# Decoder layer on one core: scores in three one-pass products, denominators on four column tiles with reciprocals spread by DMA

## The chip, the cores and the metric

The kernel runs on one core of a Trainium2 chip. The metric is the device time of one execution in microseconds, the median of several runs. The engines named below are TensorE (PE in the profile, its weight loads PEld), VectorE (DVE), ScalarE (ACT), GpSimd (POOL) and SyncE (SP), which here only issues DMAs. PSUM has eight banks of 512 fp32 columns.

## The reference

A decoder layer in fp32 on x of shape (4, 256, 128): local attention, cross-attention to a context of 512 tokens, and a mixture of experts. The change lies in the last two.

```python
# cross-attention: 16 heads of 64, b = 4, n = 256 queries, s = 512 keys
lat = layer_norm(latents, ln_lat_g, ln_lat_b)
ctx = layer_norm(context, ln_ctx_g, ln_ctx_b)
q = (lat @ Wq).reshape(b, n, HEADS, DHEAD).transpose(0, 2, 1, 3)
k, v = jnp.split(ctx @ Wkv, 2, axis=-1)          # then by head
k = apply_rope(k, cos[None, None], sin[None, None])
attn = jnp.einsum('bhnd,bhsd->bhns', q, k) * scale
attn = jax.nn.softmax(jnp.clip(attn, -11.0, 11.0), axis=-1)
out = jnp.einsum('bhns,bhsd->bhnd', attn, v)
return out @ Wo + bo
# mixture: 12 experts, three routings of the same address
x_addr = x_flat @ P_w.T
dw1, dw2, dw3 = (_route_dense(x_addr @ U.T, 3, 1.0) for U in (U1, U2, U3))
h = jax.nn.gelu(_apply_mixture(x_flat, dw1, W1), approximate=False)
y = _apply_mixture(h, dw2, W2) + dw3 @ b2
```

## The kernel before, in words

Everything is one program with one hand-written instruction list per engine; semaphores order them, and each engine runs its list in order. After the local attention come 32 rounds of cross-attention (`for r in range(NPAIR)`), one for each pair of heads of a batch entry (8 pairs each, `PPB`), then 24 expert steps (12 of the first, 12 for the second weights), then the second mixture.

One round r, on each engine:

- TensorE: the scores of the next pair (`scores`, line 1171: for two context tiles and both heads a fp32 product on 64 rows, so two row tiles), a unit of values and later a unit of rotated keys for a coming group (`unit`, line 981, three one-pass products), every other round the queries of two pairs (`queries`, lines 1104 to 1106, three one-pass products), the value products of this pair (`weigh_values`, line 1188), the sum of the weights over the context (`sum_weights`, line 1198, a product with ones, one 64-column tile for each head, so that the sum stands on all 64 rows of its head), at times the output projection (`project`, line 1207), and the transposes of the keys of pair r + 3 (`turn_keys`, line 1090).
- ScalarE: the exponents (line 806), and the copies of keys and queries out of bank 6 (lines 785 and 798), which free that bank (`misc_read`).
- VectorE: `divide(r - 1)` (reciprocal of the sums, line 1596, then the product into o_t, line 1600), the clips of the next pair (line 1589), and the rope products of the round's key unit (lines 1471 and 1476), which free bank 5 for TensorE's next unit.
- GpSimd: the sums of the weights over context tiles (lines 541, 547) and the sum of the rope products (line 533).

fp32 operands are multiplied as two records each with its own weight load; operands of type fp32r in one. Where the kernel uses fp32r it keeps fp32 accuracy by three products of a rounded first part (hi) and the rest (lo): hi·hi, hi·lo, lo·hi.

From round 22 on the routing of the first half of the tokens is worked in between (`route_1`), at fixed rounds (`ROUTE`). The routed bias dw3 @ b2 is made in the expert steps by `bias`, in steps that the table `BIAS` names: a transpose of dw3 into bank 7, ScalarE's copy (line 918), and in a later step the product (line 1353). SP's list is in order too: after the loads of the start and pw, u and b2 it issues the expert weights (line 470) into a ring of four.

In `local_values` (line 1049) each of four column tiles gets two products in a row before the next tile's two:

```python
for i in range(WG):
    for half in range(2):
        mm = pe.matmul(psum[QT * i:QT * i + QT, o, at:at + G * DE]...,
                       prT[:, q:q + QT], vbd[:, NBP * b + n, :, half, :], ...)
```

Of the kernel before, what the change touches and what calls it, by code (L numbers as in the profile page):

```python
# [7 lines left out]
P = 128  # L8
# [15 lines left out]
def decoder_layer(nc, x, ctx_in, pos, a_wq, a_wk, a_wv, a_wpost, a_wrel, a_pds,  # L24
# [75 lines left out]
    with ExitStack() as ctx:  # L100
# [38 lines left out]
        def bank(i, parts=P):  # L139
# [76 lines left out]
        q_t = sb("q_t", [P, 2, QH // 2, S], F32, second)  # L216
        kT = sb("kT", [P, 3, SC], F32, second)
        e_sb = sb("e_sb", [P, ERING, 2, KH, S], F32, second)
        v_sb.append(sb("v_sb1", [P, KC, HG, DX], F32, second))
        e_part = sb("e_part", [P, 2, 2, 2, S], F32, second)  # L220
        rden = sb("rden", [P, 2, S], F32, second)
        o_t = sb("o_t", [P, 2, PPB, S], F32, second)
        second.close()
# [48 lines left out]
            xn1_done lat_in_done lat_ps lat_f_done lat_hi_done lat_lo_done bo_added             k_rot_done misc_ps misc_read score_ps exp_done  # L272
            clip_done part_done es_done pv_ps den_ps rden_done ox_done tail_ps x2_done ld_w0 ld_w1 ld_w2 ld_w3
            ld_pw ld_u ld_b2 wt_done wt_hi_done wt_lo_done rt_ps rt_done fn_done fT_ps fT_done addr_ps addr_done z_ps
            z_done fill_done top_done top3_done zr_done chosen_done zsh_done ez_done wsum_done nm_done ctx_nm_done
            dw_done pick_done spread_done gate_src_done gate_stored ld_gate0 ld_gate1 dw1_ps dw1_hi_done dw1_lo_done dw3_ps dw3_done spread_ps xe_done xe_pool_done
# [28 lines left out]
        LATENT_ROUNDS = {1: (0, 1, 2), 2: (6, 7, 8), 3: (14, 15, 16)}  # L305
# [19 lines left out]
        MISC_NO = {what: n for n, what in enumerate(MISC)}  # L325

# [10 lines left out]
        NORM_ROUND = (B - 1) * PPB - 2  # L337
        ROUTE = {"weights": 2 * NORM_ROUND, "tokens": 2 * NORM_ROUND + 2, "address": 2 * NORM_ROUND + 4, "scores": 2 * NORM_ROUND + 6,
# [16 lines left out]
        BIAS = {10: ("turn", 0), 11: ("product", 0), 13: ("turn", 1), 14: ("product", 1)}  # L355
# [18 lines left out]
        def _(sp):  # L374
# [103 lines left out]
        def _(pool):  # L478
# [110 lines left out]
            for r in range(NPAIR):  # L589
# [14 lines left out]
                if r == FILLED:  # L604
# [4 lines left out]
                    pool.tensor_tensor(pick[:, :], ident[0:SPLIT, 0:NE], ident[0:SPLIT, REST:SPLIT], ALU.add).then_inc(s["pick_done"], 1)  # L609
                    pool.wait_ge(s["pick_done"], 1)  # L610
# [18 lines left out]
        def _(act):  # L629
# [151 lines left out]
            def keys_turned(p):  # L781
# [3 lines left out]
                act.activation(kT[:, p % 3, :], bank(MISC_BANK), ACT.Copy).then_inc(s["misc_read"], 1)  # L785
# [8 lines left out]
            def queries_out(j):  # L794
# [3 lines left out]
                act.activation(q_t[:, j % 2, :, :], bank(MISC_BANK).rearrange("p (a t) -> p a t", t=S), ACT.Copy).then_inc(s["misc_read"], 1)  # L798
# [134 lines left out]
        def _(pe):  # L933
# [225 lines left out]
            def scores(i):  # L1159
# [32 lines left out]
            def sum_weights(p):  # L1192
# [4 lines left out]
                for a in range(2):  # L1197
                    mm = pe.matmul(psum[DX * a:DX * a + DX, pv_bank(p), S:2 * S], ones[:, :], e_part[:, p % 2, 0, a, :],  # L1198
                                   start=True, stop=True)
# [83 lines left out]
            for r in range(NPAIR):  # L1283
# [14 lines left out]
                if r % 2 == 0 and r // 2 + 1 < NQ:  # L1298
                    queries(r // 2 + 1)
                route_1(2 * r)  # L1300
                weigh_values(2 * r)
# [94 lines left out]
        def _(dve):  # L1396
# [154 lines left out]
            def output_bias(pair):  # L1551

                dve.wait_ge(s["ld_bo"], 16)
                for t in range(4 * pair, 4 * pair + 4):
                    dve.tensor_tensor(x_sb[:, t, :], x_sb[:, t, :], bo_all[:, :], ALU.add).then_inc(s["bo_added"], 1)  # L1555
# [20 lines left out]
            latents(0, 2)  # L1576
            local_residual(1)
            latents_lo(0)
            context_normalize(1)
            for b in range(2, B):  # L1580
                context_offset(b)
            local_normalize(4)
# [8 lines left out]
            def divide(p):  # L1591
                b, hp = divmod(p, PPB)
# [238 lines left out]
```

## Time and profile before

| | us |
|---|---|
| median of 3 runs (lowest, highest) | 453.61 (452.78, 457.39) |
| profiled execution, its own time | 453.26 |
| its span in the trace | 451.3 |
| TensorE busy | 422.7 (94%) |
| VectorE busy | 331.1 (73%) |
| GpSimd busy | 256.3 (57%) |
| ScalarE busy | 195.1 (43%) |
| mean granted clock of TensorE | 0.992 |

The span runs from the first to the last instruction of the trace; the execution's own time has some 2 us around it. Busy times are averages over stages with different limits, so the rows further down are read by stage and by round. A record of TensorE overlaps with its neighbours: its length is its latency, and the distance of two starts is what it costs in a row of them.

### The profile page before, as it was taken

The page shows a single profiled execution, that of the slowest core. Times are in us where ns is not written, and L with a number is a line of the kernel's source. Part 1 is how long each engine was busy: PE and PEld are TensorE (multiplying, and loading weights), DVE is VectorE, ACT ScalarE, POOL GpSimd, SP SyncE. Part 2 cuts the span into 40 slices and gives each one's busy share as a digit, 9 for nine tenths or more (in the row PEclk, how much of TensorE's full clock was granted, in tenths as well). Part 3 has the DMA queues.
Part 4 walks back from the last instruction along what each step waited for, and adds up shares of the span by engine and source line. Part 5 has one row for each costly group of instructions (what it writes and reads, how often), then busy time and mean ns, then how long its engine had stood idle before and what let it go on. Part 6 is the DMA issues. An engine that isn't in the chain of part 4 may idle for free.

```text
span 451.3 us, 8472 instructions
## 1 busy us (share of the span) xinstructions
PE 422.7 (94%) x3168; PEld 309.8 (69%) x3168; DVE 331.1 (73%) x692; ACT 195.1 (43%) x312; POOL 256.3 (57%) x225
## 2 busy tenths in 40 slices
PE   3998889999999999998998999999989899999996
PEld 2666666676766766666765666768756788888885
DVE  8798668989997667987685697797667861655554
ACT  6758364664654454554354363535436533100000
POOL 5758258987898768886875745677524571000000
PEclk9999999999999999999998999999999899999999
DMA  7676314000000000000000000536438640000000
GB/s 182 173 169 86 81 33 70 0 1 1 0 2 1 1 1 1 0 1 2 0 2 1 1 1 1 163 49 139 78 83 170 140 71 1 6 6 13 6 6 14
DMA packets 75434, 19.85 MB, mean 44 GB/s; under 512 B 66741, under 2 KB 73834, under 8 KB 75394
## 3 DMA queue, kind: packets, MB, share of 16 engines
q1 hardware_dynamic: 72628, 18.27, 19.1%
q10 hardware_dynamic: 2766, 1.04, 1.0%
q8 instruction: 26, 0.43, 0.4%
q14 instruction: 14, 0.11, 0.1%
HBM read 17.27 MB, written 2.02 MB: 43 GB/s over the span
## 4 chain that ended last, share of the span: by engine, by line
PE 72%; DVE 13%; issue 5%; ACT 4%; SPq 4%; DMA 1%; POOL 1%; DVEq 0%; ACTq 0%; POOLq 0%
PE psum L1188 12%; PE psum L1171 9%; PE psum L981 8%; PE psum L1371 5%; PE psum L1372 5%; PE psum L1370 5%; PE psum L1330 4%; PE psum L1332 4%; PE psum L1331 4%; PE psum L1207 3%; PE psum L1198 3%; SPq L388 3%; PE psum L1090 3%; DVE rden L1596 1%; DVE x_sb L1555 1%
## 5 line engine op out<-in xcount | busy, mean ns | idle before, releaser
L541 POOL TENSOR_TENSOR e_part<-e_sb 128x512 f32<-128x512 f32 x64 | 88.6, 1401 | 43.1 <-DVE e_sb L1589 31.1
L806 ACT ACTIVATE e_sb<-psum 128x1024 f32<-128x1024 f32 x64 | 62.2, 1021 | 16.7 <-PE psum L1171 16.7
L1188 PE MATMUL psum<-e_sb,v_sb 128*64 128x256 f32 x512 | 64.2, 391 | 0.8 <-ACT v_sb L713 0.8
L1171 PE MATMUL psum<-q_t,kT 64*128 64x256 f32 x512 | 64.2, 389 | 0.0
L1795 DVE SCALAR_TENSOR_TENSOR x_sb<-psum,dw,x_sb 128x128 f32<-128x128 f32 x96 | 33.7, 351 | 38.1 <-PE psum L1372 35.5
L1589 DVE TENSOR_SCALAR e_sb<-e_sb 128x1024 f32<-128x1024 f32 x64 | 54.0, 879 | 4.6 <-ACT e_sb L806 4.6
L1596 DVE RECIPROCAL rden<-psum 128x256 f32<-128x256 f32 x32 | 55.9, 1747 | 0.3 <-PE psum L1198 0.2
L785 ACT ACTIVATE kT<-psum 128x512 f32<-128x512 f32 x32 | 19.1, 597 | 83.1 <-PE psum L1090 82.8
L1171 PEld LDWEIGHTS psum<-q_t,kT 64*128 64x128 f32 x512 | 46.7, 186 | 9.6 <-issue 5.0
L533 POOL TENSOR_TENSOR k_rot<-rope_a,rope_b 128x512 f32<-128x512 f32 x32 | 42.2, 1321 | 18.3 <-DVE rope_b L1476 18.3
L1188 PEld LDWEIGHTS psum<-e_sb,v_sb 128*64 128x64 f32 x512 | 34.7, 138 | 23.2 <-issue 6.2
L581 POOL TENSOR_TENSOR xeT_lo<-xeT,xeT_hi 128x512 fp32r<-128x512 f32 x24 | 31.4, 1309 | 33.8 <-ACT xeT_hi L820 33.6
L547 POOL TENSOR_TENSOR e_part<-e_part 128x512 f32<-128x512 f32 x32 | 41.4, 1293 | 2.5
L1471 DVE TENSOR_TENSOR rope_a<-psum,cos_sb 128x512 f32<-128x512 f32 x32 | 22.0, 687 | 26.2 <-PE psum L981 24.1
L1330 PE MATMUL psum<-xeT_hi,w1T_hi 128*128 128x512 f32 x96 | 39.5, 412 | 0.7 <-ACT h_f L926 0.3
L1332 PE MATMUL psum<-xeT_hi,w1T_lo 128*128 128x512 f32 x96 | 38.1, 397 | 0.0
L1371 PE MATMUL psum<-w2T_lo,h_hi 128*128 128x512 f32 x96 | 38.0, 396 | 0.0
L1331 PE MATMUL psum<-xeT_lo,w1T_hi 128*128 128x512 f32 x96 | 38.0, 396 | 0.0
L1372 PE MATMUL psum<-w2T_hi,h_lo 128*128 128x512 f32 x96 | 37.8, 394 | 0.0
L1370 PE MATMUL psum<-w2T_hi,h_hi 128*128 128x512 f32 x96 | 37.3, 389 | 0.0
L981 PE MATMUL psum<-wkv_hi,ctx_hi 128*128 128x512 f32 x64 | 31.6, 494 | 4.2 <-DVE rope_b L1476 4.2
L820 ACT ACTIVATE xeT_hi<-xeT 128x512 fp32r<-128x512 f32 x24 | 15.2, 632 | 36.9 <-DVE xeT L1636 22.1
(195 smaller groups left out, 774.8 us busy)
## 6 DMA issues: line engine op xcount, KB each, us to landing
w_raw<-in_L_ffn_W_dram SPq DMA_DIRECT2D x96, 64.0 KB, 2.3
gates<-gate_dram SPq DMA_DIRECT2D x6, 768.0 KB, 4.6
ctx_sb<-in_ctx_dram SPq DMA_DIRECT2D x4, 256.0 KB, 6.0
vbd<-v_dram SPq DMA_DIRECT2D x16, 52.6 KB
v_dram<-v_tok SPq DMA_DIRECT2D x4, 136.0 KB, 2.9
raw<-in_L_xattn_Wkv_dram SPq DMA_DIRECT2D x2, 256.0 KB, 4.6
k_rot<-in_L_xattn_Wkv_dram SPq DMA_DIRECT2D x2, 256.0 KB, 4.3
k_rot<-in_L_xattn_Wq_dram SPq DMA_DIRECT2D x2, 256.0 KB, 5.5
```

Of the source, the lines that this page charges most:

```text
L541: pool.tensor_tensor(e_part[:, p % 2, half, :, :], e_sb[:, i % ERING, :, 0, :], e_sb[:, i % ERING, :, 1, :], ALU.add)\
L806: act.activation(e_sb[:, i % ERING, :, :, :].rearrange("p a k t -> p (a k t)"), psum[:, a:a + 2, :].rearrange("p a b -> p (a b)"), ACT.Exp ...
L981: mm = pe.matmul(o, c, w_[:, wc:wc + GC], start=(part == 0), stop=(part == 2))
L1171: mm = pe.matmul(psum[:, 2 * (i % 2) + a, t * S:(t + 1) * S], kT[rows, p % 3, kt * P:(kt + 1) * P], q_t[rows, j % 2, p % 2, :], start=True ...
L1188: mm = pe.matmul(psum[DX * a:DX * a + DX, pv_bank(p), 0:S], v_sb[g % 2][:, kt, 2 * pp + a, :], e_sb[:, i % ERING, a, t, :], start=(kt == 0 ...
L1330: pe.matmul(bank(c), w1T_hi[:, e, c, :], hi, start=(e == 0), stop=False)
L1331: pe.matmul(bank(c), w1T_hi[:, e, c, :], lo, start=False, stop=False)
L1332: mm = pe.matmul(bank(c), w1T_lo[:, e, c, :], hi, start=False, stop=(e == NE - 1))
L1370: pe.matmul(o, hi, w_hi, start=(c == 0), stop=False)
L1371: pe.matmul(o, hi, w_lo, start=False, stop=False)
L1372: mm = pe.matmul(o, lo, w_hi, start=False, stop=(c == HC - 1))
L1596: dve.reciprocal(rden[:, p % 2, :], psum[:, pv_bank(p), S:2 * S]).then_inc(s["rden_done"], 1)
```

## The change

1. Scores: keys and queries are kept as a first part (kT_hi, q_hi, fp32r, copied by ScalarE) and the rest (kT_lo, q_lo, made by VectorE, which then frees bank 6). Each score product becomes three one-pass products.
2. Denominators, for the first 24 pairs (`QUARTERS`): the product with ones goes to four 32-column tiles, one for each head and half of the queries, 128 columns each; VectorE takes the reciprocal of 128 columns instead of 256 (`reciprocals`), SP copies each quarter to its two places by eight DMAs, and `divide`, now after the clips, waits for them.
3. The latents of batch 2 go from rounds 6 to 8 to rounds 9 to 11; the addition of bo is one instruction for four tiles, in rounds 6 and 26 instead of 5 and 18; in TensorE's round the routing products stand behind the first value products; the bias products go from steps 10, 11, 13, 14 to 13, 15, 17, 19.
4. Buffers are placed anew, and one semaphore of GpSimd goes (not shown).

```diff
-        LATENT_ROUNDS = {1: (0, 1, 2), 2: (6, 7, 8), 3: (14, 15, 16)}
+        LATENT_ROUNDS = {1: (0, 1, 2), 2: (9, 10, 11), 3: (14, 15, 16)}
+        QUARTERS = (B - 1) * PPB
-        BIAS = {10: ("turn", 0), 11: ("product", 0), 13: ("turn", 1), 14: ("product", 1)}
+        BIAS = {13: ("turn", 0), 15: ("product", 0), 17: ("turn", 1), 19: ("product", 1)}
...
+            def spread_reciprocals(p):
+
+                sp.wait_ge(s["rden_done"], p + 1)
+                if p >= 2:
+                    sp.wait_ge(s["ox_done"], p - 1)
+                for a in range(2):
+                    for h in range(2):
+                        quarter = SQ * (2 * a + h)
+                        for j in range(2):
+                            sp.dma_start(rden[DX * a + SQ * j:DX * a + SQ * (j + 1), p % 2, P * h:P * (h + 1)],
+                                         rden_q[quarter:quarter + SQ, p % 2, :]).then_inc(s["rden_spread"], 16)
+
+            for p in range(QUARTERS):
+                spread_reciprocals(p)
+
...
-                act.activation(kT[:, p % 3, :], bank(MISC_BANK), ACT.Copy).then_inc(s["misc_read"], 1)
+                act.activation(kT_hi[:, p % 3, :], bank(MISC_BANK), ACT.Copy).then_inc(s["misc_hi_done"], 1)
...
-                        mm = pe.matmul(psum[:, 2 * (i % 2) + a, t * S:(t + 1) * S], kT[rows, p % 3, kt * P:(kt + 1) * P],
-                                       q_t[rows, j % 2, p % 2, :], start=True, stop=True)
+                        o = psum[:, 2 * (i % 2) + a, t * S:(t + 1) * S]
+                        hi, lo = kT_hi[rows, p % 3, kt * P:(kt + 1) * P], kT_lo[rows, p % 2, kt * P:(kt + 1) * P]
+                        pe.matmul(o, hi, q_hi[rows, j % 2, p % 2, :], start=True, stop=False)
+                        pe.matmul(o, hi, q_lo[rows, j % 2, p % 2, :], start=False, stop=False)
+                        mm = pe.matmul(o, lo, q_hi[rows, j % 2, p % 2, :], start=False, stop=True)
...
+                    if p < QUARTERS:
+                        for h in range(2):
+                            quarter = SQ * (2 * a + h)
+                            mm = pe.matmul(psum[quarter:quarter + SQ, pv_bank(p), S:S + P], ones[:, 0:SQ],
+                                           e_part[:, p % 2, 0, a, P * h:P * (h + 1)], start=True, stop=True)
+                    else:
...
-                route_1(2 * r)
                 weigh_values(2 * r)
+                route_1(2 * r)
...
+            def keys_lo(p):
+                dve.wait_ge(s["misc_hi_done"], HI_NO["keys", p] + 1)
+                if p >= 2:
+                    dve.wait_ge(s["score_ps"], 2 * (p - 1))
+                dve.tensor_tensor(kT_lo[:, p % 2, :], bank(MISC_BANK), kT_hi[:, p % 3, :].bitcast(F32), ALU.subtract).then_inc(s["misc_read"], 1)
...
             def divide(p):
                 b, hp = divmod(p, PPB)
-                dve.reciprocal(rden[:, p % 2, :], psum[:, pv_bank(p), S:2 * S]).then_inc(s["rden_done"], 1)
-                dve.wait_ge(s["rden_done"], p + 1)
+                if p < QUARTERS:
+                    dve.wait_ge(s["rden_spread"], 16 * 8 * (p + 1))
+                else:
+                    dve.wait_ge(s["rden_done"], p + 1)
...
             for r in range(NPAIR):
                 if r:
-                    divide(r - 1)
+                    reciprocals(r - 1)
+                    if r > QUARTERS:
+                        divide(r - 1)
...
+                if r % 2 == 0 and r // 2 + 1 < NQ:
+                    queries_lo(r // 2 + 1)
...
                 route_1(2 * r)
+                if r and r <= QUARTERS:
+                    divide(r - 1)
...
                     key_unit(ROUND_KEYS[r])
+                if r + 3 < NPAIR:
+                    keys_lo(r + 3)
```

What moves on VectorE, in an even and an odd round in the middle of the 32. Before, from the key unit of one round (rope_a, rope_b are the rope products) over the division and the clips (e_sb):

```order
L1471 TENSOR_TENSOR rope_a<-psum,cos_sb 128x512
L1476 TENSOR_TENSOR rope_b<-psum,sin_sb 128x8x32 x2
L1596 RECIPROCAL rden<-psum 128x256
L1600 TENSOR_TENSOR o_t<-psum,rden 128x256
L1589 TENSOR_SCALAR e_sb<-e_sb 128x1024 x2
L1471 TENSOR_TENSOR rope_a<-psum,cos_sb 128x512
L1476 TENSOR_TENSOR rope_b<-psum,sin_sb 128x8x32 x2
```

And now, with kT_lo and q_lo the rests and rden_q the half-width reciprocals:

```order
L1501 TENSOR_TENSOR rope_a<-psum,cos_sb 128x512
L1506 TENSOR_TENSOR rope_b<-psum,sin_sb 128x8x32 x2
L1611 TENSOR_TENSOR kT_lo<-psum,kT_hi 128x512
L1641 RECIPROCAL rden_q<-psum 128x128
L1634 TENSOR_SCALAR e_sb<-e_sb 128x1024 x2
L1617 TENSOR_TENSOR q_lo<-psum,q_hi 128x512
L1653 TENSOR_TENSOR o_t<-psum,rden 128x256
L1501 TENSOR_TENSOR rope_a<-psum,cos_sb 128x512
```

The division has gone from ahead of the clips to behind them and behind the rest of the queries; the rest of the keys stands between the rope products and the reciprocal.

On SP, between the loads of round 0 and the expert weights. Before:

```order
L435 DMA u_sb<-in_L_ffn_U_dram 12x64 x3
L436 DMA b_sb<-in_L_ffn_b_dram 12x128
L470 DMA w_raw<-in_L_ffn_W_dram 32x16x32 x16
L440 DMA gate_dram<-gate_src 12x512 [waits gate_src_done]
L453 DMA gates<-gate_dram 128x1536 [waits misc_ps,pv_ps,gate_stored]
```

And now (of the 24 groups of eight the first and the last):

```order
L442 DMA u_sb<-in_L_ffn_U_dram 12x64 x3
L443 DMA b_sb<-in_L_ffn_b_dram 12x128
L453 DMA rden<-rden_q 32x128 [waits rden_done]
L453 DMA rden<-rden_q 32x128 x7
...
L453 DMA rden<-rden_q 32x128 [waits ox_done,rden_done]
L453 DMA rden<-rden_q 32x128 x7
L492 DMA w_raw<-in_L_ffn_W_dram 32x16x32 x16
L462 DMA gate_dram<-gate_src 12x512 [waits gate_src_done]
```

The first sixteen weight loads, which were issued in round 0, now stand behind the last group, in round 24.

## Rows read from the trace of the kernel before

**Rows 1.** The page's busy times.

```profile
PE 422.7 (94%) x3168; PEld 309.8 (69%) x3168; DVE 331.1 (73%) x692; ACT 195.1 (43%) x312; POOL 256.3 (57%) x225
```

**Rows 2.** By stage: start:end, length, busy PE, PEld, DVE, ACT, POOL, clock, DMA share, GB/s.

```profile
73.00:257.60 184.60, 178.20 (x1271) 123.45 (x1270) 148.31 (x229) 92.12 (x136) 144.83 (x115) 0.99 0.01 2
257.60:295.60 38.00, 36.18 (x290) 25.12 (x288) 31.83 (x72) 16.39 (x23) 22.72 (x18) 1.00 0.17 50
295.60:391.00 95.40, 91.32 (x414) 71.50 (x415) 62.24 (x144) 40.85 (x74) 44.00 (x35) 0.98 0.43 86
```

**Rows 3.** Timeline of one round: start, length, engine, line.

```profile
148.91 0.69 DVE L1471 TENSOR_TENSOR rope_a<-psum,cos_sb 128x512 f32<-128x512 f32 x1 [0.41 <-PE psum L981]
149.24 2.00 PE L1171 MATMUL psum<-q_t,kT 64*128 64x256 f32 x16
149.52 0.74 DVE L1476 TENSOR_TENSOR rope_b<-psum,sin_sb 128x256 f32<-128x256 f32 x2
150.18 1.75 DVE L1596 RECIPROCAL rden<-psum 128x256 f32<-128x256 f32 x1
151.96 0.42 DVE L1600 TENSOR_TENSOR o_t<-psum,rden 128x256 f32<-128x256 f32 x1
152.30 1.28 DVE L1589 TENSOR_SCALAR e_sb<-e_sb 128x1024 f32<-128x1024 f32 x2
...
156.07 0.69 DVE L1471 TENSOR_TENSOR rope_a<-psum,cos_sb 128x512 f32<-128x512 f32 x1 [2.48 <-PE psum L981]
```

**Rows 4.** Timeline, TensorE: query products (first, last), local value products.

```profile
151.97 0.28 PE L1104 MATMUL psum<-lat_hi,wq_hi 128*128 128x256 f32 x1
...
152.55 0.28 PE L1106 MATMUL psum<-lat_hi,wq_lo 128*128 128x256 f32 x1
...
38.73 2.20 PE L1049 MATMUL psum<-vbd,prT 96*32 96x68 f32 x128 [0.33 <-ACT prT L730]
```

**Rows 5.** Groups of instructions, VectorE: busy, mean ns of one.

```profile
L1520 DVE RECIPROCAL rq<-psum 128x32 f32<-128x32 f32 x5 | 1.7, 344 | 1.6 <-PE psum L1049 1.6
...
L1596 DVE RECIPROCAL rden<-psum 128x256 f32<-128x256 f32 x32 | 55.9, 1747 | 0.3 <-PE psum L1198 0.2
...
L1622 DVE TENSOR_TENSOR w1T_lo<-psum,w1T_hi 128x512 fp32r<-128x512 f32 x12 | 8.2, 687 | 5.2 <-ACT w1T_hi L813 5.2
```

**Rows 6.** Timeline, SP's DMA issues and the last VectorE group.

```profile
63.73 0.36 SPq L436 DMA_DIRECT2D b_sb<-in_L_ffn_b_dram  x1
64.14 0.35 SPq L470 DMA_DIRECT2D w_raw<-in_L_ffn_W_dram  x1
...
7.29 0.43 SPq L402 DMA_DIRECT2D affine<-in_L_xattn_ln_ctx_g_dram  x1
7.76 0.44 SPq L402 DMA_DIRECT2D affine<-in_L_xattn_ln_ctx_b_dram  x1
...
447.80 1.51 DVE L1795 SCALAR_TENSOR_TENSOR x_sb<-psum,dw,x_sb 128x128 f32<-128x128 f32 x4 [1.24 <-PE psum L1372]
449.40 0.33 SPq L474 DMA_DIRECT2D out_dram<-x_sb  x1
```

**Rows 7.** DMA issues: count, KB each, us from issue to landing.

```profile
out_dram<-x_sb SPq DMA_DIRECT2D x8, 64.0 KB, 1.5
...
pw_sb<-in_L_ffn_P_w_dram SPq DMA_DIRECT2D x1, 32.0 KB, 2.1
```

**Rows 8.** Waits of TensorE from 295 us on, and its clock.

```profile
PE psum L1353 <- ACT dw3T L918: 1.5, 1, 1.5
PE psum L1347 <- ACT gate_src L847: 1.4, 1, 1.4
...
349.20:352.60 3.40, 1.86 (x11) 1.45 (x11) 3.04 (x5) 2.81 (x6) 1.27 (x1) 1.00 0.63 100
352.60:356.10 3.50, 3.50 (x10) 2.73 (x9) 3.40 (x8) 0.93 (x2) 2.57 (x2) 0.51 0.45 69
```

More of the change, by code:

```diff
@@ L214, in decoder_layer @@
         lat_lo = sb("lat_lo", [P, B * S], F32R, second)
-        q_t = sb("q_t", [P, 2, QH // 2, S], F32, second)
-        kT = sb("kT", [P, 3, SC], F32, second)
+        q_hi = sb("q_hi", [P, 2, QH // 2, S], F32R, second)
+        kT_hi = sb("kT_hi", [P, 3, SC], F32R, second)
         e_sb = sb("e_sb", [P, ERING, 2, KH, S], F32, second)
         v_sb.append(sb("v_sb1", [P, KC, HG, DX], F32, second))
-        e_part = sb("e_part", [P, 2, 2, 2, S], F32, second)
+        sb("awT_rest", [P, 16], F32, second)
+        kT_lo = sb("kT_lo", [P, 2, SC], F32R, second)
+        q_lo = sb("q_lo", [P, 2, QH // 2, S], F32R, second)
         rden = sb("rden", [P, 2, S], F32, second)
         o_t = sb("o_t", [P, 2, PPB, S], F32, second)
+        sb("below", [P, 7144], F32, second)
+        e_part = sb("e_part", [P, 2, 2, 2, S], F32, second)
+        rden_q = sb("rden_q", [P, 2, P], F32, second)
         second.close()
@@ L325, in decoder_layer @@
         MISC_NO = {what: n for n, what in enumerate(MISC)}
+        HI_NO = {what: n for n, what in enumerate(w for w in MISC if w[0] in ("keys", "queries"))}
         def gate_bank(n):
@@ L1553, in output_bias @@
                 dve.wait_ge(s["ld_bo"], 16)
-                for t in range(4 * pair, 4 * pair + 4):
-                    dve.tensor_tensor(x_sb[:, t, :], x_sb[:, t, :], bo_all[:, :], ALU.add).then_inc(s["bo_added"], 1)
+                ts = slice(4 * pair, 4 * pair + 4)
+                dve.tensor_tensor(x_sb[:, ts, :], x_sb[:, ts, :], bo_all[:, None, :].to_broadcast([P, 4, D]), ALU.add)
             def latents_lo(b):
@@ L1581, in _ @@
                 context_offset(b)
+            queries_lo(0)
             local_normalize(4)
@@ L1589, in clip, with reciprocals @@
                 dve.tensor_scalar(e, e, E_LO, E_HI, ALU.max, ALU.min).then_inc(s["clip_done"], 1)
-            def divide(p):
-                b, hp = divmod(p, PPB)
+            def reciprocals(p):
                 dve.wait_ge(s["den_ps"], p + 1)
@@ L1595, in divide @@
                     dve.wait_ge(s["ox_done"], p - 1)
-                dve.reciprocal(rden[:, p % 2, :], psum[:, pv_bank(p), S:2 * S]).then_inc(s["rden_done"], 1)
-                dve.wait_ge(s["rden_done"], p + 1)
+                if p < QUARTERS:
+                    dve.reciprocal(rden_q[:, p % 2, :], psum[:, pv_bank(p), S:S + P]).then_inc(s["rden_done"], 1)
+                else:
+                    dve.reciprocal(rden[:, p % 2, :], psum[:, pv_bank(p), S:2 * S]).then_inc(s["rden_done"], 1)
+            def divide(p):
+                b, hp = divmod(p, PPB)
+                if p < QUARTERS:
+                    dve.wait_ge(s["rden_spread"], 16 * 8 * (p + 1))
+                else:
+                    dve.wait_ge(s["rden_done"], p + 1)
                 if hp == 0 and b >= 2:
@@ L1709, in _ @@
             key_unit(10)
-            beside = {5: (output_bias, 0), 18: (output_bias, 1)}
+            beside = {6: (output_bias, 0), NPAIR - 6: (output_bias, 1)}
             def route_1(i):
@@ L1766, in _ @@
                 if n == 0:
+                    reciprocals(NPAIR - 1)
                     divide(NPAIR - 1)
```

26 lines of the change are left out of this document (17 added, 9 removed).

## The prediction

> **What bounds the kernel now.** I read the page's busy times first: TensorE is busy for 422.7 of 451.3 us [rows 1]. An average says little about one stage, so I then cut the span: the 24 head pairs between the value products of round 1 and those of round 25 fill 184.6 us, of which TensorE is idle for 6.4; after them come 38.0 us of attention and 95.4 us of experts [rows 2]. A round there is 184.6 / 24 = 7.69 us. The timeline of one even round [rows 3] shows who is early: VectorE starts on the key unit as soon as TensorE has made it (148.91), ends its clips near 153.6, and then waits 2.48 us for the next key unit. From rope to rope is 7.16 us, all of it TensorE. So TensorE sets the pace, and VectorE has some 2.5 us to spare. The change spends that spare time, and the question is whether it spends more.
>
> **The products (TensorE).** Scores of a pair: 16 records go as 8 pairs on two row tiles, 2.00 us from first start to last end [rows 3]. The new form has 24 one-pass products. The query products are of that kind and width: first start 151.97, last 152.55, so 0.116 us from one to the next, and 0.28 for the last [rows 4]. In pairs on the two row tiles that is 11 x 0.116 + 0.28 + 0.1 (the longer first step) = 1.66 us: 0.34 less. The sums over the context halve their columns and use four tiles, two steps in the place of two longer ones: about 0.2 less. An even round of TensorE becomes 7.16 - 0.55 = 6.6 us, an odd one about 5.9 (no queries, 6 x 0.116 less). Alone this would be worth 24 x 0.55 = 13 us.
>
> The pairing needs a choice, since three products in a row now stand on one row tile before the other tile's three. The local value products are written so as well, two products (four records) in a row on one column tile, and still 128 records of 68 columns took 2.20 us, 17 ns each [rows 4]; four in a row one after the other would take more than twice that. So tiles run on their own, and I take the full pairing. The Trainium skill (TensorE: Matmul & The Clock Gate, Part 3, The mechanism) says otherwise: matmuls start and end strictly in program order. What a failed pairing costs is worked out as a rival below.
>
> **The chain on VectorE.** In the new order VectorE does: two rope products, the rest of the keys, the half-width reciprocal, clips and the rest of the queries, then it waits for the spread reciprocals, divides, and goes to the next rope. It is in order, so the DMA trip is inside each round's loop, and nothing behind the wait can start. The parts:
> - rope products: 148.91 to 150.18, 1.27 us [rows 3];
> - rest of the keys, PSUM less SBUF, 128x512: 0.69 [rows 5], less 0.07 since VectorE's neighbours overlap (150.26 against 150.18 in rows 3): 0.62;
> - reciprocal of 128 columns: between 0.344 for 32 and 1.747 for 256 [rows 5], in a straight line 0.344 + 96 x 0.00626 = 0.95;
> - the trip: eight DMAs issued by SP one after the other. Two issues of 12 rows stand 0.41 us apart (63.73, 64.14), two of 128 rows 0.47 (7.29, 7.76) [rows 6]. The new ones have 32 rows, nearest to 12: 7 x 0.41 = 2.87. The last one lands after 1.5 (SBUF to DRAM, 64 KB) or 2.1 us (DRAM to SBUF, 32 KB) [rows 7]. No DMA of before goes from SBUF to SBUF; I take 1.5, since the 2.1 has a read of DRAM in it. Two wake-ups, SP's 0.09 (447.80 + 1.51 to 449.40, rows 6) and VectorE's, rounded to 0.1 together: 4.47;
> - the division: 151.96 to 152.30, 0.34 [rows 3].
>
> Sum: 1.27 + 0.62 + 0.95 + 4.47 + 0.34 = **7.65 us** a round. Clips (two, 1.3 us) and the query rest (0.69) lie beside the trip and cost nothing unless it is under 2 us. TensorE's 6.6 and 5.9 are shorter, so TensorE no longer sets the pace; what it gains turns into waiting for the rope. What stood after the division stays in the loop: four residual adds (0.25 each) and three latent rests (0.4 each), 2.3 us. 24 x 7.65 + 2.3 = 185.9, against 184.6: **+1.3 us**. Each 0.1 us of the trip is worth 2.4 us.
>
> The trip's price is also given by the Trainium skill (DMA: Bandwidth & Descriptors, Anatomy of one DMA): about 2.0 us fixed for any transfer, though measured on GpSimd's path. With 2.0 in the place of 1.5 the sum would be 12 us higher, an estimate from that page of the Trainium skill.
>
> **The rest.**
> - Start: the query rest (0.69) stands ahead of the first scores and the rest of keys 2 (0.69) ahead of the residual that the next unit waits for; some of it lies in idle time. +1.0, between 0 and 2.
> - Rounds 25 to 31 divide as before. TensorE saves 6 x 0.34 = 2.0; VectorE, whose routing work stands here, gets three rests of keys and one or two of queries, 2.8 us. I take 0, between -2 and +2.
> - The full-width product with bo_all becomes one instruction and stands beside the trip: 0. The w_raw loads, now behind the 24 trips on SP, are first used in round 29, some 30 us later: 0. If the trips ran over, the experts' first transposes would be late.
> - Value products ahead of the routing products: nothing to win while VectorE's loop sets the pace: 0.
> - Bias products: TensorE waits 1.4 us for the turned gates and 1.5 us for the turned bias weights [rows 8]. One step of distance becomes two, at later experts, past the busiest ScalarE stretch, so both go. Behind the second wait the granted clock is 0.51 for 3.5 us, the level of 1.2 GHz in the place of 2.4, which costs 1.7 us of full-speed work [rows 8]; in the 3.40 us ahead TensorE had been busy for 1.86. With the wait gone, that goes too. **-4.6**, between -1.5 and -4.6.
> - Clock in the rounds: TensorE now idles 1 to 1.7 us in each. The only measure of that kind is the stretch just named, 1.86 busy of 3.40, and a fall after it. If a fall comes, its 1.7 us mostly fits into TensorE's slack. +2, between 0 and 6.
>
> Sum against the profiled execution's 453.26: 453.26 + 1.3 + 1.0 - 4.6 + 2 = 453.0. The median of the runs, 453.61, is 0.35 above that execution, which I leave in the rounding: **453 us**, no change.
>
> **Rivals.**
> - A, the trip is longer, and the wait that replaces TensorE's bound is worse (slower, 0.26). Place: VectorE's division in rounds 1 to 24. With issues 0.47 apart the trip is 0.42 longer, +10 us: 463; with 2.1 us of landing as well, 5.5 us in all, +24: 477. It decides from a trip of 4.7 us on; I put it at 466. For it: of the two prices of an issue the larger is that of a full tile's 128 rows, and a landing in SBUF is the one that took 2.1. Against: the new DMAs have few rows and read no DRAM.
> - B, the trip is shorter and TensorE's gain gets through (faster, 0.23). Issues as short as SP's 0.33 [rows 6] make 2.3 us, and landing in SBUF as far below 1.5 as the other row is above it, 0.9, make a trip of 3.3 and a loop of 6.5, under TensorE's even round. Then 13 us are won in the rounds: 438 in full, 443 for half-way prices.
> - C, the row tiles don't pair (0.05). Eight groups of three then take two steps each, 16 x 0.116 + 0.38 (as above) = 2.2 us, 0.2 more than now. Rounds 1 to 24 hide it (6.6 + 0.54 is under 7.65), six later ones don't: 456. The local value products speak against it [rows 4]. It is the rule that the Trainium skill (TensorE: Matmul & The Clock Gate, Part 3, The mechanism) states.
> - D, TensorE's waits drop its clock in most odd rounds (0.09): 12 falls of 1.7 us, of which about 0.5 stays each time: 459.
>
> **Numbers.** The forecast's own case (trip 4.2 to 4.7 us) has 0.37 and spans 447 to 458. About 1% (4.5 us) is what a measurement here can tell from no change. Faster by more: all of B and a fifth of the forecast, 0.30. Slower by more: A, half of D and a little of the forecast, 0.33. Within: 0.37. For 8 in 10 the range takes in most of A and B: 440 to 471.
>
> **What would show it.** In the profile after: in rounds 1 to 24 the division waits for the DMA into rden, 1 to 3 us each time, with SP's eight issues just before; TensorE's unit of values waits for the rope products; from rope to rope 7.6 us; 24 score records in 1.7 us; half-width reciprocals near 0.95 us; no wait of TensorE in the bias products. I am wrong if the last DMA lands much sooner or later than 4.5 us after the reciprocal's end, or if the score records of the two row tiles don't start in pairs.

## The result, and the profile after

The change makes the kernel slower: **502.47 us** median of four runs (501.83 to 503.06), beside 453.74 for the kernel before on the same chip. The ratio is 1.105, 95% interval 1.100 to 1.111. The forecast was 453 with a range of 440 to 471; the measured time lies outside it. All ratios here are of undisturbed runs; the highest times of two kernels below, 470.61 and 458.97 us, are runs in a slower state of the chip. The profiled execution took 502.00 us, its span is 500.1.

These are the busy times on the page after; they answer to [rows 1].

```profile
PE 429.7 (86%) x3520; PEld 317.1 (63%) x3520; DVE 320.9 (64%) x734; ACT 197.9 (40%) x312; POOL 257.6 (52%) x225
```

No engine has much more to do. TensorE is even 7 us busier (more records, and the mean granted clock of its rounds is 0.91), yet its share falls from 94 to 86%. So something makes all of them wait. The chain of waits on the same page (share of the span, first by engine, then the first lines by line) says what:

```profile
PE 36%; SPq 22%; DVE 22%; DMA 10%; issue 7%; ACT 2%; DVEq 0%; POOL 0%
SPq L453 19%; DMA rden<-rden_q 8%; PE psum L1401 4%; PE psum L1402 4%; PE psum L1400 4%; DVE rden_q L1641 4%; PE psum L1360 4%; PE psum L1362 3%; PE psum L1361 3%; DVE rope_b L1506 3%; DVE kT_lo L1611 3%; SPq L395 3%; DVE rope_a L1501 2%; P
```

SP's issuing of the spread reciprocals (L453) and their way to landing hold 27% of the chain. They were to be some 4.5 of 7.65 us in 24 rounds. The stages, cut at the value products of rounds 1 and 25 and at the first expert product, answer to [rows 2] (start:end, length, busy times, clock, DMA share):

```profile
73.51:306.94 233.43, 186.26 (x1547) 130.16 (x1546) 128.99 (x255) 93.52 (x135) 143.07 (x115) 0.91 0.08 16
306.94:349.39 42.45, 38.04 (x338) 27.08 (x337) 36.73 (x84) 17.97 (x26) 26.04 (x20) 0.96 0.26 63
349.39:500.10 150.71, 145.96 (x658) 115.90 (x657) 93.98 (x231) 40.83 (x74) 44.35 (x34) 1.00 0.29 58
```

With the same cuts in the trace before, the gain or loss of each stage is:

| stage | before | after | difference | forecast |
|---|---|---|---|---|
| start to value products of round 0 | 66.57 | 67.02 | +0.45 | +1.0 |
| value products of round 1 to round 25 | 184.61 | 233.43 | **+48.8** | +3.3, clock included |
| round 25 to the first expert product | 38.60 | 42.45 | **+3.85** | 0 |
| experts to the end | 155.09 | 150.68 | -4.4 | -4.6 |

The whole surprise is in the rounds, 9.73 us each in the place of 7.69. One of them in the timeline answers to [rows 3]:

```profile
150.45 0.95 DVE L1641 RECIPROCAL rden_q<-psum 128x128 f32<-128x128 f32 x1
151.19 3.24 PE L1212 MATMUL psum<-e_sb,v_sb 128*64 128x256 f32 x16
151.43 4.94 SPq L453 DMA_DIRECT2D rden<-rden_q  x8
151.94 1.26 DVE L1634 TENSOR_SCALAR e_sb<-e_sb 128x1024 f32<-128x1024 f32 x2
157.57 0.42 DVE L1653 TENSOR_TENSOR o_t<-psum,rden 128x256 f32<-128x256 f32 x1 [4.37 <-DMA rden<-rden_q]
157.91 0.68 DVE L1501 TENSOR_TENSOR rope_a<-psum,cos_sb 128x512 f32<-128x512 f32 x1
158.51 0.75 DVE L1506 TENSOR_TENSOR rope_b<-psum,sin_sb 128x256 f32<-128x256 f32 x2
159.17 0.68 DVE L1611 TENSOR_TENSOR kT_lo<-psum,kT_hi 128x512 fp32r<-128x512 f32 x1
159.31 0.50 PE L1002 MATMUL psum<-wkv_hi,ctx_hi 128*128 128x512 f32 x1 [1.57 <-DVE rope_b L1506]
159.77 0.95 DVE L1641 RECIPROCAL rden_q<-psum 128x128 f32<-128x128 f32 x1
```

Read it as a circle. The reciprocal ends at 151.40; SP's eight issues fill 151.43 to 156.37; the division starts at 157.57, after VectorE has stood still for 4.37 us; then division, rope and key rest, and the next reciprocal at 159.77, 9.32 us after the last. TensorE waits for the rope (1.57 us). The value products, 1.95 us at the full 2.4 GHz in a round of the trace before, take 3.24 here: the granted clock from 151.2 to 154.4, behind a wait of TensorE, is 0.58, so most of that stretch runs at 1.2 GHz. It lies inside TensorE's own slack, since TensorE still has to wait at the end of the round. What all instructions on the spread tile show, in this one round and in the whole run (duration ns min/median/max, first and last start), is:

```profile
L453 SPq DMA_DIRECT2D rden<-rden_q x8: 507/590/592, 151.4 to 155.8; - x8
```

```profile
L453 SPq DMA_DIRECT2D rden<-rden_q x192: 507/591/1608, 73.3 to 302.5; - x192
...
  DVE o_t L1653: 97.6, 24
...
DMA to landing us min/median/max: 1.7/1.8/3.4
```

An issue takes 0.59 us, and the next one follows 0.04 later. It was to be 0.41 from start to start. All 24 divisions wait, 97.6 us together.

The forecast named its own sign of being wrong, a last landing much later than 4.5 us after the reciprocal's end; here the division starts 6.17 us after it.

The score records stand as forecast, 24 in 1.7 us, two at a time (the first three groups and the last):

```profile
156.05 0.39 PE L1194 MATMUL psum<-q_hi,kT_hi 64*128 64x256 f32 x2
156.27 0.29 PE L1195 MATMUL psum<-q_lo,kT_hi 64*128 64x256 f32 x2
156.39 0.29 PE L1196 MATMUL psum<-q_hi,kT_lo 64*128 64x256 f32 x2
...
157.45 0.29 PE L1196 MATMUL psum<-q_hi,kT_lo 64*128 64x256 f32 x2
```

In kernel.py the three products of one row tile come before the three of the other; in the trace two records of line 1194, which can only be of the two tiles, start 0.01 us apart, ahead of the second product of either. The rule that matmuls start strictly in program order (the Trainium skill, TensorE: Matmul & The Clock Gate, Part 3, The mechanism) doesn't hold between row tiles in this trace.

### The profile page after: what moved, and what is told of

Read it like the earlier page. It is cut to its first block, busy times and chain, and to the rows that moved or that the text cites. A ratio compares the mean times of both kernels' runs of the same rounds, so it can differ in the third digit from the quotient of the medians.

```text
span 500.1 us, 9474 instructions
## 1 busy us (share of the span) xinstructions
PE 429.7 (86%) x3520; PEld 317.1 (63%) x3520; DVE 320.9 (64%) x734; ACT 197.9 (40%) x312; POOL 257.6 (52%) x225
## 3 DMA queue, kind: packets, MB, share of 16 engines
HBM read 17.27 MB, written 2.02 MB: 39 GB/s over the span
## 4 chain that ended last, share of the span: by engine, by line
PE 36%; SPq 22%; DVE 22%; DMA 10%; issue 7%; ACT 2%; DVEq 0%; POOL 0%
SPq L453 19%; DMA rden<-rden_q 8%; PE psum L1401 4%; PE psum L1402 4%; PE psum L1400 4%; DVE rden_q L1641 4%; PE psum L1360 4%; PE psum L1362 3%; PE psum L1361 3%; DVE rope_b L1506 3%; DVE kT_lo L1611 3%; SPq L395 3%; DVE rope_a L1501 2%; PE psum L1212 2%; DVE e_sb L1634 1%
## 5 line engine op out<-in xcount | busy, mean ns | idle before, releaser
L563 POOL TENSOR_TENSOR e_part<-e_sb 128x512 f32<-128x512 f32 x64 | 89.9, 1424 | 43.8 <-DVE e_sb L1634 31.3
L1653 DVE TENSOR_TENSOR o_t<-psum,rden 128x256 f32<-128x256 f32 x32 | 13.6, 425 | 97.9 <-DMA rden<-rden_q 97.6
L1212 PE MATMUL psum<-e_sb,v_sb 128*64 128x256 f32 x512 | 72.4, 425 | 0.1
L806 ACT ACTIVATE kT_hi<-psum 128x512 fp32r<-128x512 f32 x32 | 19.2, 599 | 98.9 <-PE psum L1111 98.5
L1212 PEld LDWEIGHTS psum<-e_sb,v_sb 128*64 128x64 f32 x512 | 37.3, 152 | 27.7 <-issue 14.1
L1634 DVE TENSOR_SCALAR e_sb<-e_sb 128x1024 f32<-128x1024 f32 x64 | 45.0, 740 | 1.6 <-ACT e_sb L827 1.6
L1002 PEld LDWEIGHTS psum<-wkv_hi,ctx_hi 128*128 128x128 f32 x64 | 12.3, 192 | 48.4 <-DVE rope_b L1506 38.9
L1194 PE MATMUL psum<-q_hi,kT_hi 64*128 64x256 f32 x256 | 41.9, 317 | 0.3 <-DVE q_lo L1617 0.3
L1360 PE MATMUL psum<-xeT_hi,w1T_hi 128*128 128x512 f32 x96 | 38.9, 405 | 0.8 <-ACT h_f L947 0.5
L1195 PE MATMUL psum<-q_lo,kT_hi 64*128 64x256 f32 x256 | 38.5, 290 | 0.0
L1196 PE MATMUL psum<-q_hi,kT_lo 64*128 64x256 f32 x256 | 38.5, 290 | 0.0
```

The costliest lines, as they stand in the source:

```text
L563: pool.tensor_tensor(e_part[:, p % 2, half, :, :], e_sb[:, i % ERING, :, 0, :], e_sb[:, i % ERING, :, 1, :], ALU.add)\
L1002: mm = pe.matmul(o, c, w_[:, wc:wc + GC], start=(part == 0), stop=(part == 2))
L1212: mm = pe.matmul(psum[DX * a:DX * a + DX, pv_bank(p), 0:S], v_sb[g % 2][:, kt, 2 * pp + a, :], e_sb[:, i % ERING, a, t, :], start=(kt == 0 ...
L1360: pe.matmul(bank(c), w1T_hi[:, e, c, :], hi, start=(e == 0), stop=False)
L1634: dve.tensor_scalar(e, e, E_LO, E_HI, ALU.max, ALU.min).then_inc(s["clip_done"], 1)
```

## The experiments

**The theory**: eight issues of one queue, one after the other, and a landing stand inside VectorE's in-order loop and set its length. **Rivals**: the rests of keys and queries that VectorE now makes; TensorE's clock; a long landing rather than long issues.

### No quarters at all

```diff
-        QUARTERS = (B - 1) * PPB
+        QUARTERS = 0
```

With it go the DMAs, the four column tiles and the half-width reciprocals, and the division stands ahead of the clips again.

> The changed kernel with no pair in quarters: sums on 64 columns, reciprocals of 256 columns, no DMA. Theory (eight issues of SP and a landing inside VectorE's in-order loop make the 9.7 us rounds): the rounds are TensorE's again, 7.69 - 0.34 for the scores = 7.3 us or a little less, and the bias products keep their 4.6 us, so 437 to 443 us. Rival (the rests of keys and queries that VectorE now takes are what slows it): rests 0.62 + 0.7 in a loop that had 2.5 us to spare; if they were the cause the time would stay near 500. Rival (TensorE's clock falls because of three short products in the place of two): about 470.

Measured: 449.33 us (447.27 to 452.46), ratio to before 0.991 (0.987 to 0.994). The quarters as a whole cost 53 us, so neither the rests (near 500) nor the clock (470) are the cause; which part of the quarters it is, the next runs show. But the expectation was missed by 6 us at the least: the rounds 1 to 24 took 181.9 us and not 175, and the end of attention 43.0 and not 38.6. What waits for what on TensorE, in this run from 66 to 310 us (us in total, times, longest):

```profile
PE psum L1111 <- DVE q_lo L1617: 7.3, 4, 2.4
PE psum L1111 <- DVE x_sb L1660: 2.9, 1, 2.9
PE psum L1002 <- DVE rope_b L1506: 2.2, 4, 1.1
```

The first two waits are new or longer: the turned keys need the bank that the query rest frees, and in one late round they need it from a residual add that stands behind VectorE's routing work (0.5 us before). Both are followed up below.

### Dividing later

```diff
-                if r and r <= QUARTERS:
-                    divide(r - 1)
...
                 if r + 3 < NPAIR:
                     keys_lo(r + 3)
+                if r and r <= QUARTERS:
+                    divide(r - 1)
```

> Eight DMAs as in the change, but VectorE divides after the rope and the key rest, just before the next reciprocal. Then only reciprocal 0.95 + trip 6.2 + division 0.34 = 7.5 us stand in the loop, the 1.9 us of rope and key rest lie beside the trip: 24 x 1.9 to 2.2 = 46 to 53 us less than the change, 450 to 457. If SP's issues take longer when TensorE and VectorE are less idle: 460 to 470. Rival (not the place of the wait in VectorE's order, but the clock or the rests): over 490.

Measured: 461.96 us (458.77 to 464.95), ratio 1.019 (1.012 to 1.026): 40 us of the 49 come back with the same eight DMAs, by nothing but the place of the wait. The profile has the smaller wait of the division and a new one behind it, since the division also frees the bank that the next value products write:

```profile
  DVE o_t L1653: 25.1, 17
  PE psum L1212: 13.0, 12
```

From the reciprocal's end to the division's start it is 6.80 us on average, not 6.2; 0.95 + 6.80 + 0.34 = 8.09 a round, and 24 rounds took 193.6 us. So the 450 to 457 us of the theory were missed, and the time lies in the second range, 460 to 470. That range had longer issues as its reason. Against the change, whose mean is 6.49, the issues hold only 0.05 us more and the landings 0.26; why these landed later is open.

### Half of the DMAs

Only four of a pair's eight DMAs are issued from pair 2 on, and the division waits for these alone; half of rden keeps the values of pairs 0 and 1.

```diff
-                        for j in range(2):
+                        for j in range(2 if p < 2 else 1):
...
```

> From pair 2 on only four of the eight DMAs are issued (half of rden keeps values of pairs 0 and 1, so outputs differ). Theory: an issue costs 0.63 us, four less take 2.5 us out of each round: loop 7.0 to 7.3, 22 x 2.5 = 55 us less than the change, 443 to 450 us. If an issue costs what I forecast (0.41) and the rest of the trip is a fixed landing that I underrated: 22 x 1.64 = 36 less, 466. Rival (clock, rests): over 490.

Measured: 451.94 us (447.72 to 470.61), ratio 0.995 (0.992 to 0.998). Typical trips are 3.63 us, 2.54 less than the 6.17 of the change, so **one DMA less is 0.63 us less**, and it is the issues that count, not a long landing. The rounds lost 48.5 us, 22 x 2.2 and not 22 x 2.5, so the time is 2 us above the range expected: in some of them TensorE sets the pace again.

### What an issue costs, by itself

A kernel of DMAs alone, in stages of eight issues by SP and a wait.

> A kernel of DMAs alone: SP issues eight at a time and waits, SBUF to SBUF with 32, 12, 64, 128 rows of 512 bytes and 32 rows of 64 bytes, SBUF to DRAM and DRAM to SBUF with 32 rows, and one single DMA; nothing else of the reference is computed. Theory 1 (the issue's price goes by rows and by SBUF on both sides): 32 rows SBUF to SBUF 0.59 each, 12 rows 0.41, 128 rows above 0.6, and DRAM on one side cheaper at 32 rows. Theory 2 (0.59 comes from load of other engines in the full kernel): here 0.41 to 0.47 for 32 rows. Landing of the last one 1.7 to 1.9 us after its issue inside SBUF.

Measured, each row one stage; the first four are SBUF to SBUF with 32, 12, 64 and 128 rows of 512 bytes, then 32 rows of 64 bytes, then 32 rows of 512 bytes from SBUF to DRAM and from DRAM to SBUF (duration ns min/median/max):

```profile
L32 SPq DMA_DIRECT2D s<-src x8: 507/591/592, 4.4 to 8.8; - x8
L32 SPq DMA_DIRECT2D s<-src x8: 713/714/847, 10.5 to 16.0; - x8
L32 SPq DMA_DIRECT2D s<-src x8: 544/596/597, 17.8 to 22.3; - x8
L32 SPq DMA_DIRECT2D s<-src x8: 482/602/610, 24.1 to 28.5; - x8
L32 SPq DMA_DIRECT2D n<-src x8: 573/590/592, 30.4 to 34.8; - x8
L32 SPq DMA_DIRECT2D hbm<-src x8: 352/421/422, 36.5 to 39.7; - x8
L32 SPq DMA_DIRECT2D l<-in_x_dram x8: 325/422/423, 41.2 to 44.4; - x8
```

With no other engine at work an issue inside SBUF costs the same 0.591 us as in the full kernel, so it isn't load. Rows (32, 64, 128) and bytes (an eighth) move it by 2%. **With DRAM on one side it costs 0.42, with SBUF on both 0.59** (32 rows of 512 bytes). Of theory 1 the half on SBUF is right, the half on rows is wrong, and 12 rows were dearest of all. Why SBUF on both sides costs more is not shown. From the start of a stage's last issue to the next stage's first it is 1.76 us for 32 rows inside SBUF, within the 1.7 to 1.9 expected, and 1.49 to DRAM.

### Two queues

Four of a pair's DMAs are issued by ScalarE's queue, behind its copy of the value unit (and of the queries, in even rounds).

```diff
...
-                spread_reciprocals(p)
+                spread_reciprocals(sp, p, 0)
...
+                if r and r <= QUARTERS:
+                    spread_reciprocals(act, r - 1, 1)
```

> The change whole, but of the eight DMAs of a pair four are issued by SP and four by ScalarE's queue, behind its copy of the value unit. Theory (the trip is the issues of one queue, one after the other, 0.63 us each): both halves go side by side and the trip is 3.65 us as with four DMAs, the loop 7.0 to 7.7 us; 450 to 455 us. Rival (the descriptors or the engines behind them are what takes 0.6 us, whichever queue issues): trip 6.2, 500 us. In between, if ScalarE comes to its issues late: 460 to 475.

> A kernel of DMAs inside SBUF alone, nothing else of the reference is computed: eight of 32 rows to the same partitions, to the next 32, eight of 128 rows, of 12 rows, of 16 rows; then four on SP's queue and four on ScalarE's at the same time; then eight on ScalarE's alone. If each queue has its own price: 0.59 us on either, alone or side by side, and the four and four take 2.5 us together. If the queues share what takes the time: 5 us for the four and four. Same partitions or shifted ones: no difference.

Measured: 459.0 us (456.17 to 460.15), ratio 1.010 (1.007 to 1.013). Half of the trips are 3.93 to 3.97 us, so the halves do go side by side; the mean is 4.69 and the longest 7.32, where ScalarE came to its issues late. So the time lies between the two ranges expected, 450 to 455 and 460 to 475. In the kernel of DMAs alone four and four took 2.7 us together (first and second rows; the third is SP's eight to the same partitions, and eight to the next 32 partitions took the same 0.590 each):

```profile
34.95 2.41 SPq L27 DMA_DIRECT2D both<-src  x4
34.96 2.70 ACTq L27 DMA_DIRECT2D both<-src  x4
```

```profile
L27 SPq DMA_DIRECT2D same<-src x8: 586/590/592, 2.6 to 7.0; - x8
```

Spreading DMAs over engines brings no bandwidth, it only saves issue time: so says the Trainium skill (DMA: Bandwidth & Descriptors, Rules for kernel authors). Issue time was what was short here, and the trips of 3.96 us in the place of 6.17 agree.

### The scores back in fp32

The quarters and all moved products stay; the copies of keys and queries are whole fp32, and VectorE makes no rests of them.

```diff
-                        pe.matmul(o, hi, q_hi[rows, j % 2, p % 2, :], start=True, stop=False)
-                        pe.matmul(o, hi, q_lo[rows, j % 2, p % 2, :], start=False, stop=False)
-                        mm = pe.matmul(o, lo, q_hi[rows, j % 2, p % 2, :], start=False, stop=True)
+                        mm = pe.matmul(o, kT_hi[rows, p % 3, kt * P:(kt + 1) * P], q_hi[rows, j % 2, p % 2, :], start=True, stop=True)
...
```

> The change with its scores in fp32 as before (no rests of keys and queries on VectorE); quarters, DMAs and moved products stay. Theory: in the loop of reciprocal, trip, division, rope and key rest only the key rest goes, 0.62 us: 24 x 0.62 = 15 us, and the 3.9 us that the end of attention lost: 502.5 - 15 - 4 = 483 us, still 30 us slower than before. Rival (the rests and the DMAs get in each other's way): under 470. Rival (the rests cost nothing): 502.

Measured: 487.31 us (485.69 to 488.7), ratio 1.073 (1.070 to 1.077). The rounds lose 12.1 us of 233.4, the stretch after them 2.7: the rests are the smaller part. From the division to the next reciprocal's end it is 0.60 us less each time, near the 0.62 of the forecast; the trips were 0.15 longer on average (6.64).

### The parts that were moved

The kernel before with the bias products' new places alone (its edit is shown), and the scores alone: full reciprocals, and the latents, the routing and bias products and the addition of bo in their old rounds and order. Only the new buffers, the semaphore and the one instruction for four tiles of bo stay.

```diff
-        BIAS = {10: ("turn", 0), 11: ("product", 0), 13: ("turn", 1), 14: ("product", 1)}
+        BIAS = {13: ("turn", 0), 15: ("product", 0), 17: ("turn", 1), 19: ("product", 1)}
```

> The kernel before with only the bias products' new places. Theory: the waits of 1.4 and 1.5 us in the bias products and the low clock behind the second go: 4.6 us less, 449 us, and from the first expert product to the end 150.6 us (155.1 before). Rival (the other changes brought those 4.4 us): 453.5.

> Only the scores as three products; full reciprocals, and latent, routing, value and bias products in their old places. Theory: 4.4 us of the 4.2 that the change without quarters is faster than before (449.3 against 453.5) are the bias products; the scores win 0.33 a round on TensorE and lose as much to VectorE's rests: 452 to 455 us. Rival (scores worth 24 x 0.33 = 8 us and more): 445.

Measured: bias alone 449.0 us (447.88 to 449.56), ratio 0.989 (0.986 to 0.992); scores alone 452.84 (450.14 to 458.97), 0.998 (0.995 to 1.000). The experts' stage of the first has the length and the clock that it has in the change:

```profile
296.73:447.40 150.67, 145.95 (x658) 115.89 (x657) 93.16 (x231) 40.58 (x74) 44.46 (x34) 1.00 0.29 58
```

So as much as the change without quarters wins (449.3) is won by the bias products alone, and the scores alone win 0.2%, within the noise. By stages the other moves aren't without effect: with the scores alone rounds 1 to 24 take 185.7 us and the stretch from round 25 to the experts 38.1, with the moves as well (no quarters) 181.9 and 43.0. They win about 4 us in the rounds and lose 5 behind them. These are single profiled executions; the kernel with the residual early, of the next section, has 181.9 too.

### Mending the two new waits

Without quarters, VectorE adds the residual ahead of the routing work; then, besides, the query rest stands between the two clips.

```diff
+                if r in extras and extras[r][0] == "project":
+                    add_projected(extras[r])
                 route_1(2 * r)
                 if r and r <= QUARTERS:
                     divide(r - 1)
-                if r in extras:
-                    if extras[r][0] == "latents":
-                        latents_lo(extras[r][1])
-                    else:
-                        add_projected(extras[r])
+                if r in extras and extras[r][0] == "latents":
+                    latents_lo(extras[r][1])
```

```diff
                     clip(2 * r + 2)
+                if r % 2 == 0 and r // 2 + 1 < NQ:
+                    queries_lo(r // 2 + 1)
+                if r + 1 < NPAIR:
                     clip(2 * r + 3)
...
-                if r % 2 == 0 and r // 2 + 1 < NQ:
-                    queries_lo(r // 2 + 1)
```

> The kernel without quarters (449.3 us), and VectorE adds a projected residual ahead of the routing work of its round, not behind it. Theory: in the round after value products 27 TensorE waited 2.90 us for that add, and then ran its 24 score records at half clock (3.0 us in the place of 1.7), which made the stretch from value products 25 to the experts 4.4 us longer than before the change. With the add early both go: 3 to 4.5 us less, 445 to 446.5, and that stretch is 38.5 to 40 us. Rival (the three rests of keys and one of queries on VectorE, 2.8 us, bind there whatever the order): 449, no gain.

> As the one with the residual early, and the rest of the queries stands between VectorE's two clips, not behind both. Theory: without quarters TensorE waits four times, 7.3 us in all, for the query rest to free the bank into which the keys are turned; 0.7 us earlier takes some 2.5 us of that away, and the low clock behind the two long waits: 2.5 to 5 us less than the other, 440 to 444 us. Rival (the second clip is late by the same 0.7 us and the value products wait for it instead): the same time as the other.

Measured: 446.62 us (443.27 to 447.14), ratio 0.982 (0.979 to 0.986), and **442.42 us (441.43 to 443.53), ratio 0.975 (0.972 to 0.977)**. The second beats the kernel before by 2.5%, and by the medians the change by 12%. First the kernel without quarters around the late residual: the turned keys wait 2.90 us, and the scores behind them run at a clock of 0.50, 1.2 GHz.

```profile
276.21 0.28 DVE L1660 TENSOR_TENSOR x_sb<-psum,x_sb 128x128 f32<-128x128 f32 x1
276.63 1.09 PE L1111 MATMUL psum<-ident,k_rot 128*128 128x128 f32 x4 [2.90 <-DVE x_sb L1660]
```

```profile
276.63:280.50 3.87, 3.87 (x28) 3.33 (x28) 2.11 (x2) 1.62 (x2) 0.83 (x1) 0.50 0.00 0
```

With the residual early the same place reads:

```profile
272.91 0.29 DVE L1660 TENSOR_TENSOR x_sb<-psum,x_sb 128x128 f32<-128x128 f32 x1
273.12 1.02 DVE L1737 TENSOR_TENSOR chosen<-chosen,ez 128x144 f32<-128x144 f32 x1
273.34 0.63 PE L1111 MATMUL psum<-ident,k_rot 128*128 128x128 f32 x4 [0.47 <-DVE x_sb L1660]
```

The stretch from round 25 to the experts went from 43.0 to 38.9 us, as expected. With the query rest earlier too, TensorE's wait for it fell from 7.3 to 3.4 us and the rounds from 181.9 to 177.1, at full clock; the stretch behind them took 0.9 more. These are that run's stages:

```profile
72.32:249.46 177.14, 169.03 (x1455) 121.35 (x1455) 159.63 (x256) 90.53 (x135) 140.29 (x115) 1.00 0.02 3
249.46:289.31 39.85, 36.63 (x338) 25.96 (x338) 37.75 (x84) 17.74 (x26) 24.95 (x20) 1.00 0.16 48
```

### Quarters with every mend

Two queues, the division behind rope and key rest, and both orders of the section above.

> Quarters with every mend: two queues, the division behind rope and key rest, the residual early, the query rest between the clips. Theory: reciprocal 0.95, trip 3.65 and division 0.34 make 4.9 us, less than TensorE's 6.15 and 6.85, so TensorE sets the pace again, with sums 0.17 us shorter: up to 24 x 0.17 = 4 us under the same kernel without quarters (442.4): 438 to 443 us. Rival (ScalarE's own issues, 2.5 us a round, make the next scores' exponentials late): 445 to 455.

Measured: 443.51 us (443.26 to 444.15), ratio 0.978 (0.975 to 0.980). The divisions wait 0.8 us in all:

```profile
  DVE o_t L1654: 0.8, 1
  PE psum L1213: 0.6, 2
```

The DMAs are hidden at last, and nothing is won with them: with full reciprocals it was 442.4, and the intervals of the two ratios overlap. Time on VectorE that the half-width reciprocal saves is worth nothing while TensorE sets the pace, and the 0.17 us a round that the sums save on TensorE did not show: rounds 1 to 24 took 178.3 us against 177.1.

## Why the prediction was wrong

**The failed step** is the trip's first term: "The new ones have 32 rows, nearest to 12: 7 x 0.41 = 2.87." I ordered the prices of an issue in [rows 6] by rows. The DMAs in them all have DRAM on one side, and in the rows measured here that is what the price went by (12 rows inside SBUF, at 0.71, aside): seven steps of 0.62 are 4.35 us. The prediction had noticed that no DMA of before goes from SBUF to SBUF, but used it only for the landing. Nor did the upper bound hold, a trip of 5.5 us: it too came from rows with DRAM in them, and so was no bound for another kind.

The trip, term by term (in us; the last column is times 24):

| | forecast | measured | in 24 rounds |
|---|---|---|---|
| first issue to last | 2.87 | 4.35 | +35.5 |
| wake-ups and landing | 1.6 | 1.82 | +5.3 |
| single issues of up to 1.6, landings of up to 3.4 | 0 | 0.32 (mean 6.49, typical 6.17) | +7.7 |

Together 48.5; with the forecast's own +1.3 that is +49.8, and +48.8 was measured. The rest of the loop was right: typically 3.15 us from the division's start to the next reciprocal's end against 3.18, with the reciprocal at 0.95 and the key rest as said, and 2.9 us in all for what else stood there, against 2.3. The mechanism was right too, and named: VectorE's order puts the trip into each round. Each 0.1 us of it was said to be worth 2.4 us: 2.02 us more of it make 48.5, and the rounds took 47.5 more than the 185.9 of the sum.

**The landing** took 1.79 us from the last issue's start to the division, between my 1.5 and the 2.0 that the Trainium skill (DMA: Bandwidth & Descriptors, Anatomy of one DMA) has as fixed cost on GpSimd's path. Both spans hold an issue, of 0.59 us here and of 0.33 in the store to DRAM from which the 1.5 came ([rows 6], [rows 7]): behind the issue's end it is 1.2 us either way. So this term was missed by the price of the eighth issue too, and not by the landing.

**Rivals.** A (a longer trip) is what happened, but its worst case, 477, stood on the same wrong bound. B (a shorter trip) is out. C (no pairing) is out by the timeline. D, the clock: it fell, to 0.91 over the rounds, and cost them little, since the trips and the typical 3.15 us leave only the 2.9 us above, and 2.3 of them were forecast as other work: little of the 2 us put on for the clock is left. It did cost where TensorE's wait stood on the critical path, as behind the late residual.

**The end of attention** was put at 0, between -2 and +2, and was +3.85. I had counted VectorE's new 2.8 us and not asked who stands behind them on that engine: the residual add that TensorE's next transposes wait for, so that a wait of 0.5 us (first row, before) became one of 2.9 (second, after), with a low clock behind it. Moving that one add gave it all back.

```profile
PE psum L1090 <- DVE x_sb L1607: 0.5, 1, 0.5
```

```profile
PE psum L1111 <- DVE x_sb L1660: 2.9, 1, 2.9
```

But the rests alone don't make that wait. The kernel with the scores alone has them all, and there it is 0.5 us (first row) and the stretch 38.1; with the moves and no rests (the scores back in fp32) it is 1.2 (second row) and 39.8; with both, 2.9 and 42.5. So two more terms put at 0 were wrong here: the addition of bo "stands beside the trip", but round 26, where it now stands, has no trip, and it takes VectorE 1.16 us (third row, after) shortly ahead of the routing work; and the value products ahead of the routing products. What each of the two does was not taken apart.

```profile
PE psum L1111 <- DVE x_sb L1660: 0.5, 1, 0.5
```

```profile
PE psum L1111 <- DVE x_sb L1655: 1.2, 1, 1.2
```

```profile
316.98 1.16 DVE L1585 TENSOR_TENSOR x_sb<-x_sb,bo_all 128x512 f32<-128x512 f32 x1
```

**The bias products** gave 4.4 of the 4.6 forecast, and alone in the kernel before 4.4 us of that stage and 4.8 of the median (453.76 to 449.0). **The start** lost 0.45, within its bounds.

**TensorE's saving** of 0.34 us a round for the scores was there (rounds of 6.15 and 6.85 us without quarters, 6.47 and 7.18 before), but VectorE's order had to be mended in two places before more than half of it showed in the time (442.4 against the 449.0 of the bias products alone, 6.6 of 32 x 0.34 = 10.9 us).

## What to carry to other kernels

Price a DMA issue by rows with the same kind of memory at either end, and if the trace has no row of that kind, say that there is no bound rather than take one from another kind; a small measurement of eight issues settles it. A chain of small DMAs on one queue inside an in-order engine's loop costs issues times count, so first move the wait behind the work that doesn't need it (40 of 49 us here), then split the queue (43 us by itself), and ask last whether the saved engine time is on the path at all. When an engine with slack is given more work, go through what stands behind it: here 0.7 us subtractions ahead of a bank's release, and subtractions and moved work together ahead of a residual add, became waits of up to 2.4 and 2.9 us on the engine that sets the pace, with half the clock behind the second. And a term that "stands beside" something costs nothing only in rounds that have that something.

## What was not expected of the hardware

- An issue inside SBUF takes 0.59 us for 32, 64 or 128 rows, and 0.71 for 12 rows (both kernels of DMAs alone); 16 rows took 0.59. Why 12 are dearer was not looked into.
- Single issues took up to 1.6 us in the full kernel (7 of the 192 over 0.7). In the kernels of DMAs alone none took over 0.9. What stretches them stays open.
- Queues are not wholly independent: SP's stores to DRAM took 0.43 us an issue alone, and 0.58 at the median while ScalarE's queue issued inside SBUF (that run's rows, SP and ScalarE):

```profile
L41 SPq DMA_DIRECT2D out_dram<-full x8: 352/578/618, 38.9 to 42.8; - x8
...
L27 ACTq DMA_DIRECT2D single<-src x8: 514/612/617, 38.9 to 43.3; - x8
```

- Three products in a row on one row tile pair fully with three on the other, 0.117 us from pair to pair.
